# A windowed-attention and feed-forward stack on one core: the token shift as two transfers, the score mask written by ScalarE, and new orders of work on all engines

## What is computed

```python
def attn_layer(x, Wqkv, qs, ksc, Wo):
    q, k, v = jnp.split(x @ Wqkv, 3, -1)          # 16 heads of 64
    q = l2norm(q) * qs;  k = l2norm(k) * ksc      # then rotary tables
    out = local_attention(q, k, v)                # a key at most 32 tokens back
    return out @ Wo
def ffn_layer(x, g, bln, W1, b1, W2, b2):
    xn = (x - mu) / jnp.sqrt(var + 1e-05) * g + bln
    a, gate = jnp.split(xn @ W1 + b1, 2, -1)
    return a * jax.nn.gelu(gate, approximate=False) @ W2 + b2
for i in range(DEPTH):                            # DEPTH = 6
    x = attn_layer(shift_tokens(x), ...) + x
    x = ffn_layer(shift_tokens(x), ...) + x
```

## Time and profile before

| | |
|---|---|
| Timed executions | 1918.3, 1936.04, 7699.03 us |
| The profiled execution's own time | 1925.6 us |
| Its span, first to last instruction | 1923.8 us |
| Mean granted clock of PE | 0.928 |
| PE busy | 1577.6 us, 82% |
| DVE busy | 1382.6 us, 72% |
| POOL busy | 1263.7 us, 66% |
| ACT busy | 1251.0 us, 65% |
| Transfers of the token shift on the chain that ended last | 17% |

### The profile page before, as it was taken

One profiled execution on the slowest core, in us unless ns is written; L12 is line 12 of the kernel. 1 busy time (PEld: TensorE's weight loads), 2 busy tenths in 40 slices (PEclk: granted clock), 3 DMA queues, 4 the chain that ended last, 5 costly groups with the idle time before them and its releaser, 6 DMA issues.

```text
span 1923.8 us, 67850 instructions
## 1 busy us (share of the span) xinstructions
PE 1577.6 (82%) x28560; PEld 1265.7 (66%) x28656; DVE 1382.6 (72%) x2564; ACT 1251.0 (65%) x4601; POOL 1263.7 (66%) x1492
## 2 busy tenths in 40 slices
PE   7588978888879789879789888797898787987974
PEld 5366766766767567667567676676676676766753
DVE  4686876876867778678868777786687686776752
ACT  3376766767757667667667676586676675775761
POOL 2487666776766767667758667676677586776640
PEclk8698989989989999999999899998898998999997
DMA  3011111012111011111111211111211101111110
GB/s 108 13 35 57 39 50 40 26 52 60 35 40 40 27 52 48 43 51 32 40 49 34 60 39 44 30 37 40 60 37 52 41 24 41 42 37 30 36 29 28
DMA packets 50157, 80.61 MB, mean 42 GB/s; under 512 B 8227, under 2 KB 16086, under 8 KB 49854
## 3 DMA queue, kind: packets, MB, share of 16 engines
q1 hardware_dynamic: 49854, 76.27, 14.1%
HBM read 18.62 MB, written 1.05 MB: 10 GB/s over the span
## 4 chain that ended last, share of the span: by engine, by line
PE 46%; DMA 18%; DVE 15%; POOL 9%; ACT 8%; issue 5%; SPq 0%; DVEq 0%; POOLq 0%
DMA xsh<-xr 17%; PE ps L393 6%; PE ps L439 5%; PE ps L449 5%; PE ps L386 5%; ACT pr L647 4%; PE ps L480 4%; PE ps L409 3%; PE ps L388 3%; PE ps L387 3%; DVE t L946 3%; DVE t L948 3%; POOL t L795 3%; PE ps L420 2%; ACT sq L610 2%
## 5 line engine op out<-in xcount | busy, mean ns | idle before, releaser
L776 POOL TENSOR_TENSOR t<-t 128x512 f32<-128x512 f32 x384 | 486.9, 1280 | 86.6 <-DVE t L948 85.4
L647 ACT ACTIVATE pr<-ps,nmax 128x64 f32<-128x64 f32 x1536 | 460.1, 344 | 0.9 <-DVE nmax L963 0.9
L795 POOL TENSOR_TENSOR t<-t,rn 128x512 f32<-128x512 f32 x384 | 397.2, 1056 | 7.5
L393 PE MATMUL ps<-consts,t 128*128 128x128 f32 x1536 | 245.3, 295 | 148.3 <-POOL t L795 138.4
L647 ACT ACTIVATION_READ_ACCUMULATOR pr<-ps,nmax 128x1 f32 x1536 | 364.5, 238 | 0.0
L946 DVE TENSOR_TENSOR t<-ps,rope 128x512 f32<-128x512 f32 x384 | 262.9, 685 | 106.1 <-PE ps L393 74.5
L393 PEld LDWEIGHTS ps<-consts,t 128*128 128x128 f32 x1536 | 192.3, 151 | 204.5 <-POOL t L795 155.8
L610 ACT ACTIVATE sq<-ps 128x512 f32<-128x512 f32 x384 | 230.8, 616 | 107.4 <-PE ps L388 101.1
L386 PE MATMUL ps<-w_hi,xt_hi 128*128 128x512 f32 x576 | 272.2, 473 | 25.6 <-DVE t L948 9.1
L806 POOL TENSOR_TENSOR pr<-pr,rsum 128x512 f32<-128x512 f32 x192 | 201.9, 1052 | 104.0 <-DVE rsum L970 104.0
L948 DVE TENSOR_TENSOR t<-ps,rope 128x512 f32<-128x512 f32 x384 | 261.2, 680 | 0.0
(11 more groups left out here) (122 smaller groups left out, 2732.6 us busy)
## 6 DMA issues: line engine op xcount, KB each, us to landing
v_win<-v SPq DMA_DIRECT2D x384, 128.0 KB, 2.4
wqkv<-wqkv_in SPq DMA_DIRECT2D x36, 256.0 KB, 4.1
xsh<-xr SPq DMA_DIRECT2D x24, 254.0 KB
wo<-wo_in SPq DMA_DIRECT2D x6, 512.0 KB, 14.6
w<-w_in SPq DMA_DIRECT2D x6, 342.0 KB, 4.5
w<-w_in SPq DMA_DIRECT2D x6, 172.5 KB
x<-x_in SPq DMA_DIRECT2D x4, 256.0 KB, 3.9
out<-x SPq DMA_DIRECT2D x4, 256.0 KB, 7.3
```

Of the source, the lines that this page charges most:

```text
L393: i = tr(ps[:, TQ_BANK[c], k * P:(k + 1) * P], t1[:, c, k * P:(k + 1) * P], ident)
L647: i = A(pr[:, c, odd * SPAN:(odd + 1) * SPAN], ps[:, S_BANK[odd], c * SPAN:(c + 1) * SPAN], ACT.Exp, bias=nmax[:, odd, c:c + 1], accum_out ...
L776: G.tensor_tensor(t1[:, c, :], t1[:, c, :], t2[:, c, :], ALU.add).then_inc(qk_added[c], 1)
L795: G.tensor_tensor(w, w, rn[:, par(u), h2, a, :].unsqueeze(2).broadcast_to([P, 8, E]), ALU.mult).then_inc(done, 1)
```

## The change

It has three parts. The token shift becomes two DMAs, partitions 0 to 111 and 112 to 126, counted on the same semaphore. The two mask matmuls of each unit go; ACT copies `band16` into both score banks instead (`mask_scores`), after the exponentials of the unit before, and PE waits for it. And the order within `step` is laid out anew on all five engines, with other banks and waits to fit.

```diff
+SHIFT_PARTS = [(0, 112), (112, 15)]
...
-                sp.dma_start(xsh[1:P, :, :], xr[0:P - 1, s, :]).then_inc(f_shifted, 16)
+                for t, n in SHIFT_PARTS:
+                    sp.dma_start(xsh[t + 1:t + 1 + n, :, :], xr[t:t + n, s, :]).then_inc(f_shifted, 16)
...
-                for odd in range(2):
-                    mm(ps[:, S_BANK[odd], :], ident16[:], band16[:].rearrange("p c w -> p (c w)"), start=True, stop=False,
-                       skip_group_check=True)
+                pe.wait_ge(band_ready, u + 1)
...
+            def mask_scores(u):
+
+                if u == 0:
+                    act.wait_ge(const_ready, 9)
+                else:
+                    act.wait_ge(exp_ready[3], u)
+                band = band16[:].rearrange("p c w -> p (c w)")
+                A(ps[:, S_BANK[0], :], band, ACT.Copy)
+                A(ps[:, S_BANK[1], :], band, ACT.Copy).then_inc(band_ready, 1)
...
-                pool.wait_ge(f_shifted, 16 * (f + 1))
+                pool.wait_ge(f_shifted, 16 * len(SHIFT_PARTS) * (f + 1))
...
             def step(s):
-                run(s, 2, normalise_q, 1)
-                run(s, 2, normalise_k, 1)
...
+                run(s, 0, rotate, Q0)
+                run(s, 0, rotate, K0)
+                run(s, 0, lower_w, K0)
+                run_quad(s, 6, copy_half)
+                run(s, 0, refine_norm)
+                run(s, 0, normalise_q, 0)
```

More of the change, by code:

```diff
@@ L383, in project @@
             def project(u, c):
+                if c == Q0:
+                    pe.wait_ge(xt_ready, u // QUAD + 1)
                 w = slice(CHUNK_COLS[c], CHUNK_COLS[c] + 512)
@@ L555, in step @@
                     scores(s - 1)
+                if live(s, 2):
+                    bank_free_of_input(s, 14)
+                    weigh_values(s - 2)
+                if due(s, 10):
+                    bank_free(s, (rope_done[Q1], 0), (rope_done[Q1], 1), (rope_done[Q1], 2), (rope_done[Q1], 3), (rope_done[Q1], 4), (rope_done[Q1], 5), (rope_done[Q1], 6), (rope_done[Q1], 7))
+                    bank_free_of_quad(s, f_h, 10, FCH, -2)
+                    ffn_up_value((s - 10) // QUAD, 2)
+                if due(s, 8):
+                    bank_free(s, (rope_done[K1], 0), (v_ready[0], 1), (v_ready[0], 2), (v_ready[0], 3), (v_ready[0], 4), (v_ready[0], 5))
+                    ffn_up_gate((s - 8) // QUAD, 1)
+                if due(s, 8):
+                    bank_free_of_quad(s, f_gate, 8, FCH, -2)
+                    ffn_up_gate((s - 8) // QUAD, 2)
+                if live(s, 0):
+                    bank_free(s, (rope_done[K1], 0))
+                    bank_free_of_quad(s, f_gate, 8, FCH, -1)
+                    project(s - 0, V1)
             pe.wait_ge(ld_const, 80)
@@ L938, in rotary @@
             def rotary(u, c):
-                dve.wait_ge(sq_ready[c], u + 1)
-                if u >= 1 and c in (Q0, Q1):
+                if c in (Q0, K0, Q1):
+                    dve.wait_ge(sq_ready[c], u + 1)
+                if u >= 1 and c == Q1:
                     dve.wait_ge(tq_ps[c], u)
@@ L1029, in step @@
             def step(s):
-                run_quad(s, 7, ffn_stats)
-                run_quad(s, 8, ffn_affine)
-                run(s, 3, copy_o, 0)
-                run(s, 2, inverse_sum, 0)
-                run(s, 1, lower_w, V0)
                 run(s, 0, rotary, Q0)
                 run(s, 0, lower_w, Q0)
+                run(s, 0, sum_squares, Q0)
+                run(s, 0, rotary, K0)
+                run(s, 1, lower_w, V0)
+                run(s, 3, add_residual)
+                run_quad(s, 8, ffn_lower)
+                run_quad(s, 10, ffn_gated, 0)
+                run(s, 2, inverse_sum, 1)
+                run(s, 0, sum_squares, K0)
+                run_quad(s, 10, ffn_gated, 1)
+                run_input(s, 14, lower_xt)
                 run(s, 0, rotary, Q1)
@@ L1039, in step @@
                 run(s, 0, sum_squares, Q1)
-                run_quad(s, 8, ffn_lower)
-                run_quad(s, 9, ffn_gated, 2)
-                run(s, 2, inverse_sum, 1)
-                run(s, 3, add_residual)
-                run(s, 0, sum_squares, Q0)
-                run(s, 0, rotary, K1)
-                run_quad(s, 9, ffn_residual)
-                run(s, 0, sum_squares, K1)
-                run(s, 0, rotary, K0)
-                run_input(s, 9, lower_xt)
-                run(s, 0, sum_squares, K0)
-                run(s, 0, clamp_norm)
+                run(s, 0, sum_squares, K1)
+                run(s, 0, clamp_norm)
+                run(s, 0, rotary, K1)
                 run(s, 1, row_max)
-                run_quad(s, 8, ffn_gated, 0)
+                run_quad(s, 10, ffn_gated, 2)
                 run_quad(s, 7, ffn_normalise)
-                run_quad(s, 8, ffn_gated, 1)
                 run(s, 0, copy_v, 1)
+                run_quad(s, 6, ffn_stats)
+                run_quad(s, 7, ffn_affine)
                 run(s, 0, copy_v, 0)
+                run(s, 0, copy_qk, Q0)
+                run_quad(s, 12, ffn_residual)
+                run(s, 1, inverse_sum, 0)
                 run_layer(s, -8, rope_tables, 1)
```

194 lines of the change are left out of this document (89 added, 105 removed).

## The result

The changed kernel took 1849.18 us (median of four runs, 1844.81 to 1861.96) beside 1938.53 for the kernel before: a ratio of 0.9581, 95% interval 0.9504 to 0.9658. The 1938.53 is the median of four executions, and the one of 7699.03 us among them is left out of the ratio, as is in every ratio here an execution well above the others of its kernel. The forecast was 1655 us, and 1849 lies outside its range of 1595 to 1765. The profiled execution took 1861.96 us, its span 1860.2.

The account below looks back on a forecast made before the run. The shift's stall was taken to bound the kernel, PE next; a quad of 75.3 - 8.9 - 1.5 - 1.0 = 63.9 us, 23 times, and 9 us at the end gave 1925.6 - 262 - 9 = 1655 us, range 1595 to 1765.

Parts of the forecast that it names:

- What bounds the kernel: POOL's copy behind the token shift: one DMA engine carries the transfer, stalling the path 8.9 us a quad; PE bounds next.
- The shift in two: Token shift: two transfers land in about 3.9 us instead of 13.9, so the stall goes, -8.9 us a quad.
- The mask on PE: Two mask matmuls removed from each unit on PE: -1.5 us a quad.
- The mask on ACT: Two mask copies added on ACT: counted as 0, hidden by idle time; 4 us a quad without that.
- The feed-forward work: Feed-forward work spread over three steps fills some of PE's gaps: -1.0 us a quad, between 0 and 4.8.
- the rest of the order: Copies swapped between ACT and DVE, and SP's `shift_v` queued behind a shift: 0.
- The end: The last copy's wait for the shift, with nothing else left, shortens by 9 us.
- The third rival: ACT's list: the mask's 4 us a quad show and spreading gives nothing, 1804 us; chance 0.12.
- PE packs tightly: Rival: PE alone nearly sets the pace, with a quad of 60 us, 1565 us in all; chance 0.08.
- POOL waits for the norm: Rival: POOL idles longer for ACT's guess ahead of the refinement, making the kernel slower, 1976 us; chance 0.03.
- The shift doesn't get faster: Rival: both pieces together take as long as one transfer, POOL stalls as before, 1868 or 1891 us; chance 0.04.
- Two marks of my own list: Listed signs: ACT busy about 100 us more; POOL's idle time for the shift under 30 us, off the chain's head.

Follow-up runs that it names:

- e1: The kernel before, in its old order, with the token shift split into two transfers and nothing else changed: 1734.92 us, ratio 0.901.
- e11: The kernel before with the shift in two and the two mask matmuls left out (scores without a mask): 1709.07 us, ratio 0.8879.
- e5: The kernel before with the shift in two and the mask copied by ACT after the copy of K1: 1792.15 us, ratio 0.9316.
- e10: The changed kernel without any mask, neither copies on ACT nor matmuls on PE: 1790.31 us, ratio 0.9286.
- e17: The changed kernel with three of four normalising operations on DVE left out in each quad: 1812.17 us, ratio 0.9438.
- e18: The old order with the split shift and three of four normalising operations on DVE left out: 1727.78 us, ratio 0.8971.
- e13: The changed kernel with PE's transposes of the normalised quad behind V0 and Q0's transposes, and further moves to fit them in: 1893.65 us, ratio 0.9833.
- e16: The changed kernel with e13's move, DVE's feed-forward residual moved into the next step, and the mask on PE: 1901.18 us, ratio 0.9897.
- e6: The changed kernel with the projection V1 moved between the scores and the weighing: 1886.82 us, ratio 0.9797.
- e7: The old order with the split shift and V1 between scores and weighing in three steps of four: 1721.46 us, ratio 0.8941.

## Why the prediction was wrong, step by step

**What bounds the kernel: right.** The stall for the shift was on the path, one engine carried the transfer, and the split took it away.

**The shift in two: right, a little too large.** 8.9 us a quad forecast, 7.6 in e1; 213 us with the end, 189 measured. The landing at 2.5 us was better than the 3.9 taken. By the rule of the Trainium skill (DMA: Bandwidth & Descriptors, "Why a DMA increments its semaphore by 16 and not by 1") one engine carries 127 rows, 16 carry 112 and 15 carry 15. The landings of 13.9, 2.5 and 2.2 us agree with it.

**The mask on PE: right.** 1.5 us a quad forecast; 26 us in all in e11, 1.1 a quad.

**The mask on ACT: the first step that failed.** It was "counted as 0; what hides it is ACT's idle time". It costs 83 us in the old order (e5 less e11), 3.5 us a quad, and 59 in the new (the changed kernel less e10), 2.5 a quad. The price named for the case without cover, 4 us, was the measured one. ACT does idle for 22 us in a quad, but not between the exponentials and the mask of a unit: the chain above has ACT back to back there in the new order, and in the old one e5 has PE waiting 49 us for the copy queued behind the mask. The sum of idle time said nothing on whether it lay where the copies were put. The third rival had this mechanism and gave 1804 us, at a chance of 0.12; the measured time is 45 us above it.

**The feed-forward work and the rest of the order: the second step that failed.** -1.0 us a quad was taken for the one and 0 for the other; the new order without mask costs 81 us more than the old, +3.4 a quad. Plain steps are equal (14.7 and 14.8), so it is in the steps with feed-forward work, where the forecast saw gaps of PE to be filled. That the sum is lost there is shown; why is shown only in part. Of the 81, DVE's normalisation, slower beside POOL's long operations, accounts for some 20 to 30 (e17 and e18), uncertain by about 20. For the rest no cause is shown. The trace names two candidates that no run tested: PE's wait of 18 us for the load of `wo`, and the clock. PE's mean granted clock is 0.948 in e10 and 0.970 in e11; PE is busy for 19 us more over nearly the same matmuls, so as an estimate the clock adds at most about that much work. The two moves tried in e13 to e16 won nothing. Whether PE's stalls take part stays open, as e6 brought other waits with it.

**The end: the term did not reach the changed kernel.** 9 us were forecast. From the last row maximum to the end the kernel before takes 57.4 us and e1 44.7, but the changed kernel 59.6: its feed-forward work for the last quad lies further behind.

**The sum with measured terms**, for a quad: -7.6 (split) -1.1 (mask off PE) +2.5 (mask onto ACT) +3.4 (order) = -2.8. The terms chain from one run to the next, from e1 over e11 and e10 to the changed kernel, so that they add up is no proof of them. The copies of the shift gave 72.3 - 75.3 = -2.9 (75.3 in the earlier trace rows).

**The rivals.** "PE packs tightly" and "POOL waits for the norm" did not come: POOL's wait for the guess fell from 132.2 us to 93.8, 1.0 in a unit. "The shift doesn't get faster" fell with the landings. The Trainium skill's advice against two transfers to disjoint partitions (DMA: Bandwidth & Descriptors, "Rules for kernel authors") doesn't hold here: e1 against the kernel before is this cut and nothing else, and it is worth 10%. The advice supposes a whole that is spread over all engines.

**Two marks of my own list misled.** ACT busy for about 100 us more (91) and no wait for the shift both came, and neither says that the gain is there. The clock said part of it: forecast above 0.95, it was 0.924 where the split alone has 0.966. But it tells the orders apart and not the mask, as e5 with the mask on ACT has 0.969. The forecast of 64 us between copies failed plainly, and the prediction named who waits for the mask as the first place to look.

## What to carry to other kernels

Idle time of an engine covers an added operation only if it lies between the operation's neighbours on the dependent chain; find the ring that goes through it (here exponentials, mask, scores, weighing, copies) and count its members back to back before an operation is called free. When a change bundles a certain gain with a re-ordering, price and run the certain part alone: here it was worth 10% and the bundle 4%. A moved wait is only worth what runs in its place, so a re-laid order gets its own range on both sides of zero, not a small gain.

## What the runs showed of the hardware

**PE stalls in long rows of short instructions.** The scores and the weighing of a unit are together 448 short matmuls and weight loads in some 3 us, and PE stalls there for nothing that another engine is seen to do: up to 3.5 us at a time, 161 us in the kernel after and 81 in the kernel before. 0.7 us of long matmuls between the two take most of it away (e6: 39 us in all; e7: 41 where e1 has 86). The kernel's instructions come by DMA in packets of 16 KB (3.69 MB in 225):

```profile
q8 instruction: 225, 3.69, 0.8%
```

That the stall is a wait for such a packet is a guess from its place, not shown. The Trainium skill (Advanced Engine Details and Errata, "ISA Cache") gives 16 KB, 256 instructions, as the line of the instruction cache; the packets' size agrees.

**A stall can cost its length and then the clock.** After the 1.9 us in which PE stood at 924.6 us its matmuls of 512 columns ran 0.43 us apart instead of 0.23. Three windows of the kernel after (clock third from the end), the stall and what follows:

```profile
924.60:926.50 1.90, 0.07 (x6) 0.00 (x0) 0.07 (x1) 0.00 (x0) 1.90 (x3) 0.99 0.00 0
926.80:929.60 2.80, 2.80 (x8) 2.04 (x8) 0.00 (x0) 1.17 (x2) 2.72 (x3) 0.50 0.00 0
929.60:932.00 2.40, 2.40 (x10) 1.50 (x9) 0.69 (x1) 2.27 (x4) 0.11 (x1) 0.95 0.03 7
```

The granted clock is 0.50, 1.2 GHz, while PE is busy all the time; in the third window it is back at 2.4. Not every stall is followed by such a stretch: in this trace 39 of the 60 issue stalls of over 1.5 us are.

**DVE's normalisation between SBUF tiles is slower beside POOL's long operations.** Beside POOL's operations of 512 columns, in the kernel after (timelines of DVE and POOL):

```profile
905.63 3.73 DVE L1018 SCALAR_TENSOR_TENSOR xh<-xsh,mv,rstd 128x128 f32<-128x128 f32 x4
...
905.84 2.09 POOL L813 TENSOR_TENSOR t<-t,rn 128x512 f32<-128x512 f32 x2
907.89 2.60 POOL L792 TENSOR_TENSOR t<-t 128x512 f32<-128x512 f32 x2
```

and in e1 mostly beside its operations of 32 columns:

```profile
941.67 2.06 DVE L998 SCALAR_TENSOR_TENSOR xh<-xsh,mv,rstd 128x128 f32<-128x128 f32 x4
...
941.78 0.34 POOL L787 TENSOR_TENSOR nt<-nt,three_halves 128x32 f32<-128x32 f32 x1
942.20 0.26 POOL L789 TENSOR_TENSOR rn<-rn,nt 128x32 f32<-128x32 f32 x1
942.53 3.10 POOL L796 TENSOR_TENSOR t<-t,rn 128x512 f32<-128x512 f32 x3
```

Four of them take 3.7 us in the one case and 2.1 in the other. Within one kernel it is the same: in the kernel after, the 79 of 96 that ran mostly beside POOL's 512-column operations took 1.15 us (median), the other 17 about 0.34; in e1 16 ran beside them, at 1.35, and 80 did not, at 0.35. DVE's operations that read PSUM, such as `rotary`, took 0.68 us in both kernels. So an operation's price can depend on what the neighbour engine does at that moment, and moving it can double it.
